# A decoder of two layers on one core: four unrolled passes instead of a loop, and another order inside the attentions of 16 heads

## The reference

```
x += attention(norm(x))            # 16 heads of 16, causal, keys and values gated by a geometric memory ("own")
x += cross_attention(norm(x), ctx) # 16 heads, rotary, 154 keys, causal                                 ("cross")
x += ffn(norm(x))                  # quantised weights and rows, depthwise convolution of 3, silu
x += attention(norm(x))            # 16 heads of 16, all 1024 keys                                      ("second")
x += attention(norm(x), ctx)       # one head of 256, 154 keys                                          ("wide")
x += experts(norm(x))              # 16 experts, the best 2 of each row, and a shared one
```

## Time and profile before

| | us |
|---|---|
| median of three runs (lowest, highest) | 3564.23 (3563.89, 3576.64) |
| profiled execution | 3568.19 |
| its span, first to last instruction | 3566.9 |
| busy: PE / DVE / ACT / POOL | 3231.5 / 2350.4 / 1795.1 / 546.5 |
| DVE's reductions of first products, L736 (1856) | 1149.1, 0.659 each |
| ACT's exponentials, L702 (1024) | 922.1, 0.935 each |
| PE's first products, L607 (2688) | 720.2 |
| PE's experts, L1760 (2592) | 595.9 |
| output transfer, issue to landing (median of 8) | 2.9 |
| mean granted clock of TensorE | 0.932 |

### The profile page before, as it was taken

One profiled execution on the slowest core, in us unless ns is written; L12 is line 12 of the kernel. 1 busy time (PEld: TensorE's weight loads), 2 busy tenths in 40 slices (PEclk: granted clock), 3 DMA queues, 4 the chain that ended last, 5 costly groups with the idle time before them and its releaser, 6 DMA issues. The chain is left out here.

```text
span 3566.9 us, 46466 instructions
## 1 busy us (share of the span) xinstructions
PE 3231.5 (91%) x17428; PEld 1735.4 (49%) x17428; DVE 2350.4 (66%) x4375; ACT 1795.1 (50%) x2562; POOL 546.5 (15%) x990
## 2 busy tenths in 40 slices
PE   5998889999899878999999988899998998799999
PEld 3544432368644433236864444323786444432477
DVE  5864578746585557865668556785666744788566
ACT  2454636653346454665344545466434454546643
POOL 0111010014111101002411110100240111010033
PEclk8898979999989897999998989899999898889999
DMA  3222011113021201201302120110231201011023
GB/s 130 39 38 40 1 28 28 19 49 115 30 46 34 37 1 28 37 10 58 112 25 55 25 37 1 36 28 22 68 101 38 39 16 37 1 36 37 23 69 101
DMA packets 119358, 149.14 MB, mean 42 GB/s; under 512 B 25445, under 2 KB 77159, under 8 KB 118835
## 3 DMA queue, kind: packets, MB, share of 16 engines
q1 hardware_dynamic: 119115, 145.95, 17.0%
HBM read 75.46 MB, written 4.46 MB: 22 GB/s over the span
## 5 line engine op out<-in xcount | busy, mean ns | idle before, releaser
L736 DVE TENSOR_REDUCE small<-psum 128x1 f32<-128x512 f32 (+6 forms) x1856 | 1149.1, 659 | 320.2 <-PE psum L607 282.2
L702 ACT ACTIVATE work<-psum 128x1024 f32<-128x1024 f32 (+5 forms) x1024 | 922.1, 935 | 512.4 <-PE psum L634 256.3
L607 PE MATMUL psum<-work 96*128 96x512 bf16 (+4 forms) x2688 | 720.2, 338 | 94.9 <-DVE xn L754 32.6
L1760 PE MATMUL psum<-rounded_work 128*128 128x512 f32 x2592 | 595.9, 391 | 9.9 <-DVE rounded_work L1846 6.5
L630 PE MATMUL psum<-work 99*128 99x512 bf16 (+4 forms) x2048 | 588.5, 371 | 8.8 <-DMA work<-work 7.1
L607 PEld LDWEIGHTS psum<-work 96*128 96x128 bf16 x2688 | 244.2, 103 | 643.8 <-DVE small L736 362.9
L662 PE MATMUL psum<-work 128*32 128x512 f32 (+4 forms) x4480 | 542.9, 537 | 1.6 <-ACT work L702 1.4
L1760 PEld LDWEIGHTS psum<-rounded_work 128*128 128x128 f32 x2592 | 485.6, 188 | 114.2 <-DVE rounded_work L1846 8.3
L630 PEld LDWEIGHTS psum<-work 99*128 99x128 bf16 (+1 forms) x2048 | 183.1, 99 | 208.4 <-ACT work L702 55.8
L1861 ACT CAST rounded_work<-work 128x512 fp32r<-128x512 f32 x144 | 89.6, 622 | 338.9 <-DVE work L1902 317.4
L768 POOL CAST small<-small 128x16 bf16<-128x16 f32 x96 | 19.0, 198 | 1364.3 <-issue 977.7
(11 more groups left out here) (288 smaller groups left out, 3862.8 us busy)
## 6 DMA issues: line engine op xcount, KB each, us to landing
work<-work SPq DMA_DIRECT2D x320, 192.0 KB, 4.3
work<-combine SPq DMA_DIRECT2D x64, 512.0 KB, 4.0
work<-in_w_gate SPq DMA_DIRECT2D x64, 128.0 KB, 3.5
work<-in_w_up SPq DMA_DIRECT2D x64, 128.0 KB, 3.4
work<-in_w_down SPq DMA_DIRECT2D x64, 128.0 KB, 3.7
work<-in_x SPq DMA_DIRECT2D x10, 512.0 KB, 4.8
out<-x SPq DMA_DIRECT2D x8, 512.0 KB, 2.9
work<-work SPq DMA_DIRECT2D x64, 28.9 KB, 2.0
```

What stands on the lines that cost most here:

```text
L607: ins = nc.tensor.matmul(dst[:, c * n:(c + 1) * n], A.q_pair[0:ROWS, slot, h, P * i:P * (i + 1)], A.k_of(pair, h)[0:ROWS, s0:s0 + n], star ...
L702: nc.scalar.activation(probs[0:size, n % 4, :, 0:P * many], banks(2 * (n % 2), 2)[0:size, :, 0:P * many], ACT.Exp, scale=DH ** -0.5).then_ ...
L736: nc.vector.tensor_reduce(tops[:, pair % 2, places[0]:places[-1] + 1:step], src, AX.X, ALU.max) \
L1760: ins = nc.tensor.matmul(dst, a_parts[i], b_parts[j], start=start and n == 0, stop=stop and n == 2, skip_group_check=True)
```

## The change

The loop becomes a Python loop, so the code of a trip is written four times. `restart` at its end and the clearing of `out_stored` are gone; the semaphores count on over the four trips, and `Marks` keeps the values by trip. Where a trip needs something of the trip before, it waits for it by `at_before`: TensorE for the next context's landing and for ScalarE's last copy of the turned rows ahead of `turn_context`, and for VectorE's sums of output ahead of each bank in `gated_tensor`; GpSimd for the stored output (32 for each finished trip) and for the next rows. The last trip doesn't load, norm or turn next rows. `restart` ahead of the loop stays.

In `attention_plan` GpSimd's cut becomes a piece of its own, "cut", directly behind the join, while "top" now concerns TensorE, ScalarE and SyncE only. Tops of the pairs 0 to 6 keep their places. The last pair's top moves behind the third main entry that follows the last first product. And "norm" hangs on the entry of its spin instead of the next one. By hand from the lists above: in second `... F7.15.1 join7 cut7 S108 wide0 S109 V6.5 top7 wide1 ...` and `F7.5.1 S98 spin5 norm5 F7.6.0 F7.6.1 S99 F7.7.0`; in cross `... F7.2.1 join7 cut7 S22 spin4 norm4 S23 V5.0 top7 S24 ...`; in own `... F7.9.1 join7 cut7 S79 context0 V6.2 S80 top7 context1 ...`.

```diff
@@ Marks
-        self.sems, self.count = {}, {}
+        self.sems, self.count, self.trip = {}, {}, None
...
-        self.values[(name, *key)] = self.count[name]
+        self.values[(self.trip, name, *key)] = self.count[name]
...
+    def at_before(self, name, *key):
+        return self.sem(name), self.values.get((self.trip - 1, name, *key), 1)
@@ attention_plan
+LAST_TOP_LAG = 3
...
-                    firsts[-1].append(("join", pair - 1))
-    firsts[-1] += [("join", PAIRS_OF_HEADS - 1), ("top", PAIRS_OF_HEADS - 1)]
+                    firsts[-1] += [("join", pair - 1), ("cut", pair - 1)]
+    firsts[-1] += [("join", PAIRS_OF_HEADS - 1), ("cut", PAIRS_OF_HEADS - 1)]
...
             after(2, "spin", pair)
-            after(3, "norm", pair)
+            after(2, "norm", pair)
...
         plan += entry
+        if gone == len(firsts):
+            entries += 1
+            if entries == LAST_TOP_LAG:
+                plan.append(("top", PAIRS_OF_HEADS - 1))
@@ heads_gpsimd
-                if kind == "top":
+                if kind == "cut":
@@ setup_sync
-            nc.sync.sem_inc(out_stored, OUT_STORED)
@@ gated_tensor
-                x_tile("in", i, 0)
+                if m.trip and i % 2 == 0:
+                    pe.wait_ge(*at_before("out_ready", i + 1))
@@ expert_sync
-            load_next((b + 1) % B, "next")
+            if b + 1 < B:
+                load_next(b + 1, "next")
...
-            sp.wait_ge(*at("context_loaded", "next"))
@@ expert_tensor (likewise in expert_scalar and expert_vector)
+        more = lambda: m.trip + 1 < B
-            for j in range(NT // 2):
+            for j in range(NT // 2) if more() else ():
                 pe.wait_ge(*at("unit_multiplied", 2 * LAST + j // 2))
                 turn_tensor("next", j)
@@ the programs
-        def tensor_program():
+        def tensor_program(b):
+            if b:
+                pe.wait_ge(*at_before("context_loaded", "next"))
+                pe.wait_ge(*at_before("turned", "next", 3))
             turn_context()
...
-        def gpsimd_program():
-            pool.wait_ge(out_stored, OUT_STORED)
+        def gpsimd_program(b):
+            if b:
+                pool.wait_ge(out_stored, OUT_STORED * b)
+                pool.wait_ge(*at_before("x_loaded", "next"))
+                pool.wait_ge(*at_before("second_x_loaded", "next"))
...
-            sp.wait_ge(*at("filled", "own"))
-            nc.sync.sem_clear(range(out_stored.num, out_stored.num + 1))
...
-        with nc.Fori(0, B) as b:
-            tensor_program()
+        for b in range(B):
+            m.trip = b
+            tensor_program(b)
             scalar_program()
             vector_program()
-            gpsimd_program()
+            gpsimd_program(b)
             sync_program(b)
-            restart(nc, m, queues)
-        sp.wait_ge(out_stored, OUT_STORED)
+        sp.wait_ge(out_stored, OUT_STORED * B)
```

More of the change, by code:

```diff
@@ L63, in up @@
         self.count[name] = self.count.get(name, 0) + by
-        self.values[(name, *key)] = self.count[name]
+        self.values[(self.trip, name, *key)] = self.count[name]
         return self.sem(name), by
     def at(self, name, *key):
-        return self.sem(name), self.values.get((name, *key), 1)
+        return self.sem(name), self.values.get((self.trip, name, *key), 1)
+    def at_before(self, name, *key):
+        return self.sem(name), self.values.get((self.trip - 1, name, *key), 1)
 class Queue:
@@ L202, in attention_plan @@
     per_main = len([x for x in main if x and x[0][0] in ("score", "value")]) / PAIRS_OF_HEADS
-    plan, gone = [], 0
+    plan, gone, entries = [], 0, 0
     for k, entry in enumerate(main):
@@ L220, in build_program @@
         m = Marks(nc, ctx, known)
-        up, at = m.up, m.at
+        up, at, at_before = m.up, m.at, m.at_before
         sb = lambda name, *shape, dtype=F32: ctx.enter_context(nc.sbuf_tensor(name, [P, *shape], dtype))
@@ L263, in load_next @@
             for i0 in (0, NT // 2):
-                nc.sync.dma_start(x_next[:, i0:i0 + NT // 2, :], io["x"][bass.ds(b, 1), P * i0:P * (i0 + NT // 2), :].rearrange("b (i p) d -> p (b i) d", p=P)) \
+                nc.sync.dma_start(x_next[:, i0:i0 + NT // 2, :], io["x"][b:b + 1, P * i0:P * (i0 + NT // 2), :].rearrange("b (i p) d -> p (b i) d", p=P)) \
                     .then_inc(*up(X_LOADED[i0 != 0], tag, by=16))
             for i, n in enumerate(CTX):
-                nc.sync.dma_start(ctx_rows[0:n, i:i + 1, :], io["ctx"][bass.ds(b, 1), P * i:P * i + n, :].rearrange("b p d -> p b d")) \
+                nc.sync.dma_start(ctx_rows[0:n, i:i + 1, :], io["ctx"][b:b + 1, P * i:P * i + n, :].rearrange("b p d -> p b d")) \
                     .then_inc(*up("context_loaded", tag, by=16))
@@ L1725, in expert_sync @@
                 sp.wait_ge(*at("out_ready", i1 - 1))
-                nc.sync.dma_start(io["out"][bass.ds(b, 1), P * i0:P * i1, :].rearrange("b (i p) d -> p (b i) d", p=P),
+                nc.sync.dma_start(io["out"][b:b + 1, P * i0:P * i1, :].rearrange("b (i p) d -> p (b i) d", p=P),
                                   x[:, i0:i1, :]).then_inc(out_stored, OUT_STORED // 2)
-            sp.wait_ge(*at("context_loaded", "next"))
         def expert_gpsimd():
@@ L1864, in expert_scalar @@
                     nc.scalar.activation(pr[:, 1, :], pr[:, 0, :], ACT.Exp).then_inc(*up("best_exp"))
-                if u == NEXT_UNIT + 3:
+                if u == NEXT_UNIT + 3 and more():
                     root_scalar("next", 0, NT)
@@ L1925, in expert_vector @@
                 unit(u)
-                step = u - NEXT_UNIT
+                step = u - NEXT_UNIT if more() else -1
                 if 0 <= step < 4:
```

## The result

The changed kernel takes 3471.31 us (median of four runs, 3465.32 to 3474.46) against 3564.8 us before (four runs). The ratio of the means is 0.9728, 95% interval 0.9704 to 0.9753; 93.5 us by the medians, 97 by the ratio. The prediction was 3469. The profiled execution took 3470.28 us.

What follows compares the result with a forecast made beforehand. TensorE was taken to bound the kernel (busy 3231.5 of 3566.9 us); 18.7 + 9.5 + 0.4 + 25.6 + 11 + 30 = 95.2 us off 3568.2 gave 3473.0 profiled, 3469 median; own range 3455 to 3485, whole range 3445 to 3502.

Steps and rivals of the forecast that it cites:

- Trip ends: Three loop ends: 18.7 us of TensorE idle time, 9.5 of half clock behind them, 0.4 at the last trip's end.
- 9.5 us lie on the path and come back: Half-clock loss in the 10 us behind the three loop ends, on VectorE's path, is regained: 9.5 us.
- 3.9 us of jump: At each loop end, some 3.9 us of the gap come with the jump back and go when unrolled; barriers 1.2 us.
- Rival 3: Loop ends: the jump's 3.9 us stay in another form, and the slow clock; 11.7 + 9.5 us lost, 3490; chance 0.05.
- Last tops: TensorE's stalls at the last top of own, cross and second, 12 places: 25.6 us of idle time go, plus 11 of clock.
- The clock term: Half clock behind the 12 last-top stalls: 14.5 us counted, three quarters taken, 11 us; ends 0 and 14.5.
- Rival 2: Slow stretches stay because the clock follows its own observation phase more than these stalls; 11 + 9.5 us lost, 3489; chance 0.09.
- The norm: In second, TensorE's 24 stalls of 1.36 us for the norm shrink to 0.1 us each: 30 us; bounds 0 and 32.6.
- rival 1: In second, the norm's wait turns into TensorE waiting for VectorE's reductions; the 30 us do not come, 3499; chance 0.09.
- Rival 5: Slower than before: 64 norm holds of VectorE behind ScalarE's late copy; decides from 1.0 us each, 3627 at 2 us; chance 0.04.
- Which the ring covers: VectorE's 0.4 us hold at each of 64 norms was to be covered by the ring of three banks.
- Rival 4: Row transfers behind the moved last tops arrive late, half the clock's gain lost: 7 + 5 us, 3481; chance 0.06.

Runs made afterwards that it cites:

- e1: The changed kernel with the attentions' old order (last top directly behind its cut, norm one entry behind its spin): 3547.99 us, ratio 0.9937 to before.
- e6: The changed kernel with the last pair's top put back directly behind its cut: 3516.84 us, ratio 0.985 to before.
- e4: The kernel before, with nine useless products issued ahead of each last top's wait for the cut: 3554.23 us, ratio 0.9953 to before.
- e5: The changed kernel with the norm put back one entry behind its spin: 3502.81 us, ratio 0.9811 to before.
- e9: The changed kernel with spin and norm together one entry later: 3452.77 us, ratio 0.9675 to before.
- e11: The changed kernel with TOP_LAG = 6, tops of pairs 0 to 6 later (two first products in own and second, one in cross): 3527.23 us.
- e8: The changed kernel with 33 useless products filling TensorE's wait ahead of cross's first products in each trip: 3469.05 us, ratio 0.972 to before.
- e3: The kernel before with its four trips unrolled, barriers and clearing kept between them, old order: 3545.45 us, ratio 0.9929 to before.
- e7: The changed kernel with the last top behind the first main entry instead of the third (LAST_TOP_LAG = 1): 3487.92 us, ratio 0.9769 to before.

## Why the prediction was right

**Trip ends.** Predicted 28.6 us (18.7 + 9.5 + 0.4), measured 22 (e1). Idle time fell by 17.5. The three gaps and the three slow stretches are gone as forecast, but the total of half clock fell by only 3.3: in e1 other places fell instead (behind second's last top in the third trip the clock was 0.50 where it had been 1.00). At the ends themselves all of it came: VectorE's waits for the first copy of a trip, before and after, are 28.2 us shorter, and e1's are as short (42.8).

```profile
DVE work L1103 <- ACT xn L1002: 71.0, 4, 19.9
DVE work L1113 <- ACT xn L1012: 42.8, 4, 14.9
```

So "9.5 us lie on the path and come back" was right at its place and oversized for the kernel, since the clock's falls moved to other places. The split of a gap into 3.9 us of jump and the rest holds: 4.0. Rival 3 is out. So the rule of the Trainium skill ("Runtime: NRT & Kernel Launch", Instruction fetch mechanics) agrees with the runs; that the 4.0 us are fetching, no run separates from other costs of the jump.

The barriers were priced at 1.2 us by the setup; behind the issue they took 1.0. With the output's last sum and issue they leave 2.43 us of gap, which the sum had as 6.4 - 3.9 = 2.5.

**Last tops.** Predicted 25.6 + 11 = 36.6, measured 43.5 (e6), a difference that the interval doesn't exclude. The idle part was right (26.1 by the waits, 33.6 - 7.5; 28.9 in all). The clock term was the one mis-sized: I took three quarters of 14.5 us for what half clock gives back. In the kernel before, where 8 places fell, e4 prices it at 16.8 us by the ratio and 14.9 by the sums; e6, where all 12 fall, shows some 15 (43.5 - 28.9) to 20. The doubt that I drew from the Trainium skill's rule ("TensorE: Matmul & The Clock Gate", Part 1), that short stalls might not be the cause, is answered by e4: with the stall filled, and TensorE's order else as it was, the clock stays. Rival 2 falls as the cause; that the phase has a share shows in the 5 to 12 of 12 places at which the same stalls were followed by half clock.

**The norm.** Predicted 30, measured 29.6 (e5). VectorE is held 0.35 us in the timeline where 0.4 was said. The waits of first products for reductions stayed at 11.0 us (10.4 before), so rival 1 didn't come. Rival 5's holds exist, 64 of them at 0.49 us; that is below the 1.0 us from which they would have decided. "Which the ring covers" was wrong: by e9 the holds of second, 8.4 us, were paid in full (its stretch is 8.7 us shorter without them), and holds and spin waits together cost some 12. The 29.6 us are what the earlier norm brought after paying for them.

**Late rows.** TensorE's waits for row transfers are 7.1 us over four (2 us a trip was forecast). Rival 4 didn't come with three entries; e11 shows its price where a top is two products too late.

**The sum.** 97.9 us of span against 95.2 predicted. The order's share was 76 (66.6 predicted), the trip ends' 22 (28.6): two errors of 6 to 9 us that cancel. That the median came within 3 us of 3469 is in part luck. Of the signs that were named, idle time between trips, clock 1.00, the norm's wait, the cut's wait (7.5; about 8), and the length of a trip (851.9, 855.95 and 847.3; about 855) came as written. TensorE's idle time fell by 75.9 us, where under 60 would have been the sign of being wrong.

**Open.** Why the same stall of 2.20 us is followed by half clock in some trips and not in others. Trips 2 and 3 of the kernel after differ by 8.7 us with the same instructions and no difference in these waits. How e9's gain divides between holds, spin waits and clock is read from stretches of one trace each, and no run separates it.

## What to carry to other kernels

On an engine that is full to 90%, list its own waits and then look at the granted clock behind each of them: a stall can cost its own length and over half as much again (e6: 28.9 us and some 15 to 20), and three entries of independent work between a result and its use took both away. Full clock is worth something only if the work behind it is not waiting for something else (e8). An operation that is moved forward holds its engine until its operand is there: putting spin and norm together one entry further behind the value brought 19 us more, some 12 of them by the holds and waits. How far a piece can be moved is set by what follows it, a transfer of 3.5 us in this kernel, and two products too many cost 60 us.

## What the runs showed of the hardware

- The jump back of a loop cost 4.0 us on TensorE each time (gap 6.4 us with it, 2.43 without); two barriers and a clearing of semaphores took 1.0 us behind the last issue (e3).
- Stalls of 2.0 to 2.2 us ahead of the last tops were followed by half clock in 8 of 12 places (before), 9 of 12 (e1), 5 of 12 (e3) and 12 of 12 (e6), of 1.76 to 1.98 us in 8 of 8 (e7), stalls of 2.43 us in 3 of 3 (e3), of 0.75 us in 1 of 4 (e7), and stretches filled with useless products in 0 of 12 (e4).
- The clock also fell where TensorE was not idle. In each trip of the kernel after, L964 makes 32 products with only 8 columns each, and TensorE was busy without a break for 20 us ahead of them. The clock fell during them in the first and the third trip; in the others it fell 1.3 and 1.4 us behind them, when TensorE was already idle. The third trip:

```profile
1823.76 4.68 PE L964 MATMUL psum<-ident,work 128*128 128x8 f32 x32
```

```profile
1823.76:1826.12 2.36, 2.36 (x23) 2.36 (x22) 2.29 (x5) 0.59 (x2) 0.00 (x0) 1.00 0.03 7
1826.12:1830.12 4.00, 2.31 (x12) 2.22 (x11) 2.97 (x6) 3.77 (x8) 0.00 (x0) 0.50 0.85 159
```

- In trips 2 and 4 of the kernel after, the clock fell during 32 routing products with only 16 columns each, 3.4 us lost each time; in trips 1 and 3 it did not. In all four there is a wait of 1.6 us that ends 2.9 us ahead of them, so here the cause isn't separated.

```profile
1608.00 4.04 PE L1777 MATMUL psum<-router,xT 128*128 128x16 f32 x32
```

```profile
1608.00:1612.00 4.00, 4.00 (x34) 4.00 (x32) 1.51 (x2) 1.90 (x2) 2.57 (x4) 0.88 0.00 0
1612.00:1616.00 4.00, 4.00 (x11) 3.13 (x11) 3.69 (x34) 2.09 (x3) 0.00 (x0) 0.50 0.01 2
```
